# Adaptive-mix MoE feed-forward on one core: the shared branch's second layer in coarse and fine parts

## The chip, the cores and the metric

One core of a Trainium2 chip runs the whole program. The metric is device time in microseconds (us) of one execution. TensorE (PE) multiplies, VectorE (DVE), ScalarE (ACT) and GpSimd (POOL) do the elementwise work, SyncE (SP) issues most transfers. PEld is TensorE's weight load.

## The reference

There are 64 blocks of 32 rows by 512 features, so 2048 tokens. Each block's rows are first mixed by a small matrix that a conditioning network draws for it. The mixed rows xt then go through a mixture of experts with a shared branch:

```
logits = xt @ router_w + router_b            # 16 experts in 4 groups
gate   = top 2 experts per token, out of the best 2 groups
y      = sum over experts e of gate[:, e] * ((silu(xt @ w1[e] + b1[e]) * (xt @ w2[e] + b2[e])) @ w3[e] + b3[e])
z      = silu(xt @ sw1 + sb1) * (xt @ sw2 + sb2) @ sw3 + sb3      # the shared branch, 256 hidden
out    = x + y + z
```

All of it is float32. The change concerns the product with `sw3` alone, the shared branch's second layer: 2048 tokens x 256 hidden by 256 x 512.

## The kernel before, in words

Tokens are cut in 16 tiles of 128 and in 4 groups (g = 0 to 3) of 4 tiles. Each engine has one hand-written program, and semaphores join them; nothing is scheduled by a planner, so an engine's order is the order of the code.

1. *Mixing and routing (to about 58 us).* PE mixes and transposes the 16 tiles and forms the router's logits. For groups 0 and 1 and for the weights of the shared first layer, ACT copies each piece to a coarse part (type fp32r) and POOL subtracts that from the whole to get the fine part (line 454). These parts go into `x_split` and `w_split`.
2. *Shared first layer of groups 0 and 1 (58 to 80 us).* `shared_up(g, i)` on PE makes hidden block i (128 of the 256) of group g as three fp32r products for each pair of operands (coarse by coarse, coarse by fine, fine by coarse). ACT applies silu (`shared_silu`, line 808), DVE multiplies by the other half (`shared_hidden`, line 1014) and counts `up_ready` up. The result is `gs_of(g)`. Beside it DVE works out the gates and then each assignment's slot.
3. *Gates, shared second layer of the first tiles, dispatch (80 to 102 us).* PE transposes the gates, then `shared_down(0)` and tile 4 of `shared_down(1)`: for each tile two fp32 products of `gs_of(g)` with `sw3_sb` and one bf16 product with the bias rows. Then PE waits for DVE's and POOL's codes (lines 912 and 470) and makes the dispatch tables; then tiles 5 to 7, among the first transposes of gathered rows. DVE adds each finished tile (`shared_sum`, line 912), makes the tables of rows and the counts, and copies the first transposed rows (line 1129).
4. *Expert loop (102 to 209 us).* PE, DVE, ACT and POOL go through 34 tiles of assignments; POOL issues gathers (line 481) and scatters (line 487).
5. *End (209 to 257 us).* PE makes the shared first layer of groups 2 and 3 in plain fp32, then `shared_down(2)` and `shared_down(3)`. SP loads the experts' rows back. DVE's order is `shared_hidden(2)`, `add_rows(0)`, `add_rows(1)`, `shared_hidden(3)`, `add_rows(2)`, `shared_sum(2)`, `add_rows(3)`, `shared_sum(3)`. `add_rows` (line 1173) scales an expert's row by its gate and adds it: its two tensors both lie in SBUF. `shared_sum` has one tensor in SBUF and one in PSUM. For the last group ACT scales the second expert's rows (line 899) and POOL adds them (line 539).

## Time and profile before

| what | value |
|---|---|
| median of 3 runs | 260.02 us (259.42 to 263.33) |
| profiled execution | 259.11 us, span 257.2 us |
| PE busy | 241.2 us (94% of the span) |
| PE weight loads busy | 163.7 us (64%) |
| DVE busy | 148.5 us (58%) |
| POOL busy | 111.3 us (43%) |
| ACT busy | 78.7 us (31%) |

The span is the time between the first and the last event that the profiler shows; the execution's own time is 1.9 us longer. Busy shares are means over the stages above; the stages have different limits. A row of the timeline gives the start, the time to the end of the row, the engine, the line, what is written and read, and how many instructions the row holds; in square brackets stands how long the engine had been idle and what ended that.

### The profile page before, as it was taken

Reading aid. Unit: us, or ns where it says so; the run is one execution under the profiler, and the core shown is the slowest. Engines: PE = TensorE matmul, PEld = TensorE weight load, DVE = VectorE, ACT = ScalarE, POOL = GpSimd, SP = SyncE. Lnnn points to the kernel's source line nnn. Section 1 sums busy time; section 2 is a strip of 40 time slices with the busy share of each in tenths; the row PEclk is TensorE's granted clock in tenths of the full one; section 3 lists DMA queues with packets and bytes.
Section 4 is the critical chain, followed back from the end, with each engine's and each line's share of the span. In section 5 each row is a group of like instructions: output and inputs, shape, how many; then the busy total and the mean of one; then the engine's idle time right before and its main releaser. Section 6 shows DMA issues by size and latency. Waiting matters only on the chain.

```text
span 257.2 us, 3960 instructions
## 1 busy us (share of the span) xinstructions
PE 241.2 (94%) x1092; PEld 163.7 (64%) x1093; DVE 148.5 (58%) x314; ACT 78.7 (31%) x169; POOL 111.3 (43%) x135
## 2 busy tenths in 40 slices
PE   7947989899999988999999999999999999999994
PEld 6815767688877444667777777777777754444441
DVE  0599698838979979333333333334444420099895
ACT  2223345521317400233333333333333331100400
POOL 7782355421011056366666666666666331000170
PEclk9999799999999999999999999999999999999999
DMA  7998387689053946974445444455544222999965
GB/s 219 341 415 317 148 300 261 255 282 412 23 226 118 417 202 182 324 270 164 164 163 164 165 130 158 133 173 173 166 165 157 89 92 78 345 388 387 396 256 186
DMA packets 20698, 57.90 MB, mean 225 GB/s; under 512 B 2533, under 2 KB 2533, under 8 KB 20428
## 3 DMA queue, kind: packets, MB, share of 16 engines
q1 hardware_dynamic: 15084, 39.89, 42.2%
q0 software_dynamic: 5600, 17.83, 20.8%
q8 instruction: 7, 0.11, 0.2%
q14 instruction: 7, 0.06, 0.1%
HBM read 40.94 MB, written 17.30 MB: 226 GB/s over the span
## 4 chain that ended last, share of the span: by engine, by line
PE 78%; DVE 17%; issue 2%; DMA 1%; ACT 0%; DVEq 0%
PE psum L546 69%; PE psum L690 6%; DVE xT L1173 3%; DVE r L943 3%; DVE xT L912 2%; DVE xT L938 2%; PE psum L589 2%; DVE xT L953 2%; PE psum L703 2%; DMA xT<-cond_pack 1%; DVE x_early L912 1%; DVE mix_bias L940 1%; DVE xt_sb L1173 1%; DVE xt_sb L912 0%; DVE code_f L1107 0%
## 5 line engine op out<-in xcount | busy, mean ns | idle before, releaser
L546 PE MATMUL psum<-wexp,r 128*128 x272 | 68.4, 381 | 0.3 <-DVE r L1129 0.3
L546 PEld LDWEIGHTS psum<-wexp,r 128*128 128x128 f32 x272 | 48.5, 190 | 22.8 <-issue 16.8
L912 DVE TENSOR_TENSOR r<-psum,ebias 128x256 f32<-128x256 f32 x34 | 14.4, 425 | 65.0 <-PE psum L546 63.4
L487 POOL DMA_INDIRECT expert_rows<-late_region,to_row x33 | 33.4, 1011 | 33.6 <-ACT late_region L855 28.7
L481 POOL DMA_INDIRECT late_region<-xt_rows,from_row x36 | 35.3, 981 | 17.3 <-issue 10.8
L546 PE MATMUL psum<-wexp,xt_sb 128*128 x68 | 34.8, 594 | 0.0
L849 ACT ACTIVATE r<-r 128x128 f32<-128x128 f32 x34 | 10.5, 310 | 57.6 <-DVE r L912 47.6
L546 PE MATMUL psum<-xT,shared_sb 128*128 128x512 f32 x64 | 28.0, 593 | 0.0
L855 ACT ACTIVATE late_region<-psum 128x512 f32<-128x512 f32 x34 | 20.3, 598 | 13.9 <-issue 7.7
L1129 DVE COPY r<-psum 128x512 f32<-128x512 f32 x36 | 24.5, 680 | 0.0
L690 PE MATMUL psum<-ident,late_region 128*128 128x128 f32 x144 | 21.6, 273 | 1.0 <-DMA late_region<-xt_rows,from_row 1.0
L546 PE MATMUL psum<-x_split,w_split 128*128 128x512 f32 x96 | 22.3, 392 | 0.0
L546 PEld LDWEIGHTS psum<-xT,shared_sb 128*128 128x128 f32 x64 | 12.0, 190 | 15.5 <-issue 14.6
L690 PEld LDWEIGHTS psum<-ident,late_region 128*128 128x128 f32 x144 | 17.9, 141 | 5.5 <-issue 2.0
L546 PEld LDWEIGHTS psum<-x_split,w_split 128*128 128x128 f32 x96 | 17.9, 188 | 3.7
L791 ACT ACTIVATE xt_sb<-psum,mix_bias 128x512 f32<-128x512 f32 x16 | 11.0, 687 | 27.3 <-PE psum L546 14.2
L546 PE MATMUL psum<-router_sb,xT 128*128 128x16 f32 x128 | 16.2, 259 | 3.3 <-DVE xT L953 3.3
L546 PEld LDWEIGHTS psum<-router_sb,xT 128*128 128x128 f32 x128 | 16.0, 196 | 4.1 <-DVE xT L953 4.0
L454 POOL TENSOR_TENSOR x_split<-xT,x_split 128x512 fp32r<-128x512 f32 x8 | 10.2, 1279 | 14.3 <-ACT x_split L801 14.3
L953 DVE COPY xT<-psum 128x512 f32<-128x512 f32 x16 | 10.8, 690 | 7.5 <-PE psum L589 7.3
L539 POOL TENSOR_TENSOR xt_sb<-xt_sb,wexp 128x512 f32<-128x512 f32 x2 | 3.1, 1568 | 27.3 <-ACT wexp L899 27.3
L845 ACT ACTIVATE xt_sb<-psum 128x128 f32<-128x128 f32 x34 | 9.4, 278 | 15.1 <-PE psum L703 8.7
(175 smaller groups left out, 309.8 us busy)
## 6 DMA issues: line engine op xcount, KB each, us to landing
wexp<-expert_pack SPq DMA_DIRECT2D x16, 768.0 KB, 4.5
wexp<-expert_rows SPq DMA_DIRECT2D x8, 1024.0 KB, 13.1
xt_rows<-xt_sb SPq DMA_DIRECT2D x16, 256.0 KB, 2.2
x_early<-x SPq DMA_DIRECT2D x2, 1024.0 KB, 7.9
late_region<-x SPq DMA_DIRECT2D x2, 1024.0 KB, 12.5
ebias<-expert_bias SPq DMA_DIRECT2D x1, 2048.0 KB, 7.1
out_dram<-x_early SPq DMA_DIRECT2D x8, 256.0 KB, 9.3
shared_sb<-shared_pack SPq DMA_DIRECT2D x1, 1536.0 KB, 16.3
```

What stands on the lines that cost most here:

```text
L454: T.tensor_tensor(rest, whole, part, ALU.subtract).then_inc(split_ready, 1)
L481: nc.gpsimd.indirect_dma_start(out=xg[:, i % RING, :], out_offset=None, in_=xt_dram[:, :], in_offset=bass.IndirectOffsetOnAxis(ap=from_row ...
L487: nc.gpsimd.indirect_dma_start(out=y_dram[:, :], out_offset=bass.IndirectOffsetOnAxis(ap=rows_of.bitcast(U32), axis=0), in_=y_sb[:, slot, ...
L546: return nc.tensor.matmul(dst, lhsT, rhs, start=start, stop=stop)
L690: last = nc.tensor.transpose(psum[:, b, c * P:(c + 1) * P], xg[:, slot, c * P:(c + 1) * P], ident[:, :])
L791: nc.scalar.activation(xt_ring[:, t % RING, :], psum[:, t % 2, :], ACT.Identity, bias=mix_bias[:, t:t + 1]).then_inc(xt_ready, 1)
L849: nc.scalar.activation(s_sb[:, b, :], h_sb[:, b, 0, :], ACT.Silu).then_inc(s_ready, 1)
L855: nc.scalar.activation(y_sb[:, slot, :], psum[:, 6 + b, :], ACT.Copy).then_inc(y_ready, 1)
L912: return nc.vector.tensor_tensor(dst, a, b, op)
L953: V.tensor_copy(xT[:, t // GT, :, (t % GT) * P:(t % GT + 1) * P], psum[:, 2 + t % 2, :].rearrange("p (c n) -> p c n", c=C)).then_inc(xT_re ...
L1129: V.tensor_copy(xgT[:, b], psum[:, b, :].rearrange("p (c n) -> p c n", c=C)).then_inc(xgT_ready, 1)
L1173: ins = V.scalar_tensor_tensor(out=acc_tile(t), in0=rows_k[:, g, k, t % GT, :], scalar=tops[:, k, t:t + 1], in1=acc_tile(t), op0=ALU.mult, ...
```

## The change

The two fp32 products per tile of `shared_down` become six fp32r products. For each of the two hidden blocks: coarse hidden by coarse `sw3`, coarse hidden by fine `sw3`, fine hidden by coarse `sw3`. The bf16 bias product stays. The parts come from:

- `sw3_hi`: two ACT copies of 128x512, after ACT's exponential and ahead of its first silu; `sw3_lo`: two POOL subtractions, after the last of line 454.
- `gs_hi` of each group: two ACT copies of 128x512, after the gate parts (g = 0), after the last silu of group 1 (g = 1), after both silus of groups 2 and 3.
- `gs_lo` of each group: two POOL subtractions of 128x512; g = 0 and 1 ahead of POOL's share of the codes, g = 2 and 3 after its last scatter, ahead of its adds of line 539.

The parts are laid over regions that are free by then; `sw3_hi` is new memory, made free by a smaller scratch for POOL's transfers (8192 bytes of a partition in place of the default). `shared_down(g)` waits for its group's two fine blocks and for `sw3_lo`, where it had waited for `up_ready`.

```diff
--- before.py
+++ after.py
@@ -68,6 +68,20 @@
         with nc.sbuf_tensor("x_split", [P, EARLY, 2, C, GN], F32R) as x_split_sb, \
                 nc.sbuf_tensor("w_split", [P, 2, 2 * C * SHARED], F32R) as w_split_sb:
             x_split, w_split = x_split_sb[:, :, :, :, :], w_split_sb[:, :, :]
+        homes = {"wexp": 0, "ebias": 96, "shared_sb": 112, "x_early": 124, "late_region": 140, "xT": 156,
+                 "r1": 188, "xt_sb": 196}
+
+        def split_at(name, home, kb):
+
+            with nc.sbuf_tensor(f"ahead_of_{name}", [P, (homes[home] + kb) * 256], F32), \
+                    nc.sbuf_tensor(name, [P, IB, GN], F32R) as part:
+                return part[:, :, :]
+
+        gs_hi = (split_at("gs_hi0", "xT", 4), split_at("gs_hi1", "xT", 12), split_at("gs_hi2", "wexp", 68),
+                 split_at("gs_hi3", "late_region", 4))
+        gs_lo = (split_at("gs_lo0", "xt_sb", 0), split_at("gs_lo1", "xT", 8), split_at("gs_lo2", "wexp", 64),
+                 split_at("gs_lo3", "late_region", 0))
+        sw3_lo = split_at("sw3_lo", "shared_sb", 8)
         PRODUCTS = ((0, 0), (0, 1), (1, 0))
         w12_split = w_split.rearrange("p s (w c n) -> p s w c n", w=2, c=C)
         HALF = E // 2
@@ -161,6 +175,9 @@
                    + [spare[:, u * DIM:(u + 1) * DIM] for u in range(2)])
         gs_third = wexp_flat[:, NG * TOPK * GT * DIM:NG * TOPK * GT * DIM + IB * GN].rearrange(
             "p (i n) -> p i n", i=IB)
+
+
+        sw3_hi = sb("sw3_hi", [P, IB, DIM], F32R)
 
 
         ident = sb("ident", [P, P])
@@ -203,6 +220,10 @@
         half_loaded = [sem(f"half_loaded{h}") for h in range(2)]
         part_ready = sem("part_ready")
         split_ready = sem("split_ready")
+        down_part_ready = sem("down_part_ready")
+        down_split_ready = sem("down_split_ready")
+        gs_part_ready = sem("gs_part_ready")
+        gs_split_ready = [sem(f"gs_split_ready{g}") for g in range(NG)]
         b3_loaded = sem("b3_loaded")
         b3_ready = sem("b3_ready")
         consts_ready = sem("consts_ready")
@@ -452,6 +473,10 @@
                 pool.wait_ge(part_ready, u + 1)
                 whole, part, rest = split_of(u)
                 T.tensor_tensor(rest, whole, part, ALU.subtract).then_inc(split_ready, 1)
+            for i in range(IB):
+                pool.wait_ge(down_part_ready, i + 1)
+                T.tensor_tensor(sw3_lo[:, i, :], sw3_sb[:, i, :], sw3_hi[:, i, :], ALU.subtract
+                                ).then_inc(down_split_ready, 1)
             pool.wait_ge(xtT_done, NT)
             for r in range(RING):
                 pool.wait_ge(xt_stored[r], 16 * (NT // RING))
@@ -466,6 +491,13 @@
             pool.wait_ge(gate_rest_ready, 1)
             T.tensor_tensor(gate_rest, gate_rest, gate_parts[:, :, 1], ALU.subtract).then_inc(gate_rest_ready, 1)
 
+            def gs_rest(g):
+                for i in range(IB):
+                    pool.wait_ge(gs_part_ready, g * IB + i + 1)
+                    T.tensor_tensor(gs_lo[g][:, i, :], gs_of(g)[:, i, :], gs_hi[g][:, i, :], ALU.subtract).then_inc(gs_split_ready[g], 1)
+
+            gs_rest(0)
+            gs_rest(1)
             pool.wait_ge(code_base_ready, 1)
             T.tensor_tensor(tile_code[:, J_DVE:, 0, :], tile_code[:, J_DVE:, 0, :],
                             hi_code[:, J_DVE:].unsqueeze(2).to_broadcast([P, TOPK * NT - J_DVE, TW]), ALU.mult
@@ -532,6 +564,8 @@
             pool.wait_ge(to_copied, 1)
             scatter_rows(to_slot[:, 1:2], 1)
 
+            gs_rest(2)
+            gs_rest(3)
             pool.wait_ge(x_again_loaded, 16 * (NT - EARLY * GT))
             for u in range(GT):
                 t = LAST * GT + u
@@ -623,7 +657,8 @@
                             between[w, c]()
 
             def shared_down(g, tiles=range(GT)):
-                pe.wait_ge(up_ready, IB * (g + 1))
+                pe.wait_ge(down_split_ready, IB)
+                pe.wait_ge(gs_split_ready[g], IB)
                 for t in (g * GT + u for u in tiles):
                     if t == 0:
                         pe.wait_ge(gateT_ready, 1)
@@ -634,9 +669,12 @@
                     elif t in (6, 7):
                         pe.wait_ge(z_ready, t - 5)
                     bank = psum[:, DOWN_BANKS[t], :]
+                    cols = slice((t % GT) * P, (t % GT + 1) * P)
                     for i in range(IB):
-                        mm(bank, gs_of(g)[:, i, (t % GT) * P:(t % GT + 1) * P], sw3_sb[:, i, :],
-                           start=(i == 0), stop=False)
+                        whole, rest = gs_hi[g][:, i, cols], gs_lo[g][:, i, cols]
+                        mm(bank, whole, sw3_hi[:, i, :], start=(i == 0), stop=False)
+                        mm(bank, whole, sw3_lo[:, i, :], start=False, stop=False)
+                        mm(bank, rest, sw3_hi[:, i, :], start=False, stop=False)
 
                     if t == 0:
                         pe.wait_ge(b3_ready, 1)
@@ -812,6 +850,16 @@
             act.wait_ge(xtT_done, NT)
             for r in range(RING):
                 act.wait_ge(xt_stored[r], 16 * (NT // RING))
+            def gs_part(g):
+                for i in range(IB):
+                    act.wait_ge(up_ready, g * IB + i + 1)
+                    nc.scalar.activation(gs_hi[g][:, i, :], gs_of(g)[:, i, :], ACT.Copy
+                                         ).then_inc(gs_part_ready, 1)
+
+            act.wait_ge(shared_loaded, 16)
+            for i in range(IB):
+                nc.scalar.activation(sw3_hi[:, i, :], sw3_sb[:, i, :], ACT.Copy).then_inc(down_part_ready, 1)
+            act.wait_ge(split_ready, SPLITS)
             shared_silu(0)
             shared_silu(1, [0])
 
@@ -824,11 +872,13 @@
             nc.scalar.activation(gate_parts[:, :, 5], gate_parts[:, :, 0], ACT.Copy)
             act.wait_ge(gate_rest_ready, 2)
             nc.scalar.activation(gate_parts[:, :, 2], gate_rest, ACT.Copy).then_inc(gate_parts_ready, 1)
+            gs_part(0)
             for q in range(NG):
                 act.wait_ge(gateT_done, q + 1)
                 nc.scalar.activation(gateT[:, q * GN:(q + 1) * GN], psum[0:GROWS, GATE_BANKS[q], :], ACT.Copy
                                      ).then_inc(gateT_ready, 1)
             shared_silu(1, [1])
+            gs_part(1)
 
             act.wait_ge(pslot_ready, 1)
             act.wait_ge(gateT_done, NG)
@@ -890,7 +940,9 @@
             hidden_transposed(1, tiles)
             result(1, 1, tiles, count_of(act, N_SCATTERED + 2))
             shared_silu(2)
+            gs_part(2)
             shared_silu(3)
+            gs_part(3)
 
             act.wait_ge(rows_loaded[LAST], 16 * TOPK)
             for u in range(GT):
@@ -1193,7 +1245,7 @@
     import concourse.bacc as bacc
     from concourse.bass_utils import run_bass_kernel_spmd
 
-    nc = bacc.Bacc("TRN2", target_bir_lowering=False, num_devices=1)
+    nc = bacc.Bacc("TRN2", target_bir_lowering=False, num_devices=1, dynamic_dma_scratch_size=8192)
     a = {n.removeprefix("L0_").removeprefix("cond_"): np.asarray(v) for n, v in inputs.items()}
     cond, b2 = np.asarray(inputs["cond_128"]), a["b2"]
     _, out_c, in_c, _ = a["weight"].shape
```

POOL, from the last of `w_split` to the codes (before, then the change):

```order
L454 TENSOR_TENSOR w_split<-shared_sb,w_split 128x512 [waits part_ready] x4
L458 CAST xt_sb<-ebias 102x512 [waits xt_stored2,xt_stored1,xt_stored3,xt_stored0,xtT_done]
L459 CAST r<-ident 128x128
L460 IOTA xt_sb 128x128
L464 TENSOR_TENSOR late_region<-late_region 128x272 [waits gate_part_ready]
L467 TENSOR_TENSOR late_region<-late_region 128x272 [waits gate_rest_ready,gate_part_ready]
L470 TENSOR_TENSOR r<-r,hi_code 128x10x48 [waits code_base_ready]
```
```order
L475 TENSOR_TENSOR w_split<-shared_sb,w_split 128x512 [waits part_ready] x4
L478 TENSOR_TENSOR sw_lo<-shared_sb,sw_hi 128x512 [waits down_part_ready] x2
L483 CAST xt_sb<-ebias 102x512 [waits xt_stored2,xt_stored1,xt_stored3,xt_stored0,xtT_done]
L484 CAST r<-ident 128x128
L485 IOTA xt_sb 128x128
L489 TENSOR_TENSOR late_region<-late_region 128x272 [waits gate_part_ready]
L492 TENSOR_TENSOR late_region<-late_region 128x272 [waits gate_rest_ready,gate_part_ready]
L497 TENSOR_TENSOR gs_lo<-xt_sb,gs_hi 128x512 [waits gs_part_ready] x2
L497 TENSOR_TENSOR gs_lo<-xT,gs_hi 128x512 [waits gs_part_ready] x2
L502 TENSOR_TENSOR r<-r,hi_code 128x10x48 [waits code_base_ready]
```

Two subtractions for `sw3_lo` now stand ahead of the bias cast, and four for `gs_lo` ahead of the codes. The names of the tile read show the group: `xt_sb` holds group 0's hidden blocks, `xT` group 1's.

PE, from the gates' transposes into the second tile of `shared_down(0)` (before, then the change):

```order
L546 MATMUL psum<-r,late_region 102x128 [waits up_ready,ranks_read,ident_bf_ready,gate_parts_ready]
L546 MATMUL psum<-r,late_region 102x128 x15
L546 MATMUL psum<-shared_sb,xt_sb 128x512 [waits gateT_ready,up_ready]
L546 MATMUL psum<-shared_sb,xt_sb 128x512
L546 MATMUL psum<-xt_sb,xT 128x512 [waits b3_ready]
L546 MATMUL psum<-shared_sb,xt_sb 128x512 [waits gateT_ready]
L546 MATMUL psum<-shared_sb,xt_sb 128x512
```
```order
L580 MATMUL psum<-r,late_region 102x128 [waits up_ready,ranks_read,ident_bf_ready,gate_parts_ready]
L580 MATMUL psum<-r,late_region 102x128 x15
L580 MATMUL psum<-sw_hi,gs_hi 128x512 [waits gateT_ready,gs_split_ready0,down_split_ready]
L580 MATMUL psum<-sw_lo,gs_hi 128x512
L580 MATMUL psum<-sw_hi,gs_lo 128x512
L580 MATMUL psum<-sw_hi,gs_hi 128x512
L580 MATMUL psum<-sw_lo,gs_hi 128x512
L580 MATMUL psum<-sw_hi,gs_lo 128x512
L580 MATMUL psum<-xt_sb,xT 128x512 [waits b3_ready]
L580 MATMUL psum<-sw_hi,gs_hi 128x512 [waits gateT_ready]
```

Where the first tile began with `up_ready`, it now waits for the fine parts of the hidden blocks and of `sw3`, and has six products ahead of its bias product.

POOL, from its last scatter to the end (before, then the change):

```order
L531 ISA [waits y_ready]
L531 COPY to_slot<-to_row 128x1
L487 DMA expert_rows<-late_region,to_slot 4096x512 [waits to_copied]
L539 TENSOR_TENSOR xt_sb<-xt_sb,wexp 128x512 [waits last_scaled,x_again_loaded]
L539 TENSOR_TENSOR xt_sb<-xt_sb,wexp 128x512 [waits last_scaled]
L539 TENSOR_TENSOR xT<-xT,wexp 128x512 [waits last_scaled] x2
```
```order
L563 ISA [waits y_ready]
L563 COPY to_slot<-to_row 128x1
L519 DMA expert_rows<-late_region,to_slot 4096x512 [waits to_copied]
L497 TENSOR_TENSOR gs_lo<-wexp,gs_hi 128x512 [waits gs_part_ready] x2
L497 TENSOR_TENSOR gs_lo<-late_region,gs_hi 128x512 [waits gs_part_ready] x2
L573 TENSOR_TENSOR xt_sb<-xt_sb,wexp 128x512 [waits last_scaled,x_again_loaded]
L573 TENSOR_TENSOR xt_sb<-xt_sb,wexp 128x512 [waits last_scaled]
L573 TENSOR_TENSOR xT<-xT,wexp 128x512 [waits last_scaled] x2
```

The four subtractions of groups 2 and 3 come ahead of the four adds.

## Rows read from the trace of the kernel before

**Rows 1.** The page: the chain that ended last, share of the span by engine.
```profile
PE 78%; DVE 17%; issue 2%; DMA 1%; ACT 0%; DVEq 0%
```

**Rows 2.** Chain of waits from 56 to 103 us: start, us, what.
```profile
81.44 9.92 PE psum L546 x25
...
92.10 1.53 PE psum L546 x32
...
101.82 1.34 PE psum L546 x5
```

**Rows 3.** Timeline of TensorE: fp32r products, then fp32 products (two records each).
```profile
74.71 5.73 PE L546 MATMUL psum<-x_split,w_split 128*128 128x512 f32 x24
...
212.80 25.05 PE L546 MATMUL psum<-xT,shared_sb 128*128 128x512 f32 x58
```

**Rows 4.** Timeline from 57 to 92 us: VectorE, GpSimd and ScalarE on slots and codes.
```profile
57.80 0.61 POOL L458 CAST xt_sb<-ebias 102x512 bf16<-102x512 f32 x1 [4.85 <-DMA xt_rows<-xt_sb]
...
60.87 0.42 DVE L912 TENSOR_TENSOR late_region<-late_region,r 128x256 f32<-128x256 f32 x1
...
74.99 0.42 DVE L1045 COPY late_region<-psum 128x256 f32<-128x256 f32 x1 [1.41 <-PE psum L546]
...
78.39 0.46 ACT L826 ACTIVATE late_region<-late_region 128x272 bf16<-128x272 f32 x1
...
79.07 0.59 DVE L912 TENSOR_TENSOR late_region<-psum,late_region 128x256 f32<-128x256 f32 x1
...
84.19 3.35 DVE L912 TENSOR_TENSOR late_region<-xt_sb,pslot 128x3072 bf16<-128x3072 bf16 x1
...
87.45 1.75 DVE L912 TENSOR_TENSOR r<-tile_iota,late_region 128x1536 bf16<-128x1536 f32 x1
...
89.94 2.06 POOL L470 TENSOR_TENSOR r<-r,hi_code 128x480 bf16<-128x480 bf16 x1 [11.59 <-DVE r L1082]
```

**Rows 5.** Timeline near 20 us: a subtraction on GpSimd, four copies on VectorE.
```profile
18.50 0.78 DVE L943 COPY r<-xT 32x64 f32<-32x64 f32 x4
...
21.91 1.29 POOL L454 TENSOR_TENSOR x_split<-xT,x_split 128x512 fp32r<-128x512 f32 x1 [3.35 <-ACT x_split L801]
...
21.98 1.87 DVE L943 COPY r<-xT 32x64 f32<-32x64 f32 x4
```

**Rows 6.** Instructions of lines 801 and 1173: ns min/median/max, first and last start.
```profile
L801 ACT ACTIVATE x_split<-xT x8: 619/620/631, 21.1 to 41.1; 128x512 fp32r<-128x512 f32 x8
...
L1173 DVE SCALAR_TENSOR_TENSOR x_early<-wexp,tops,x_early x16: 746/747/752, 226.1 to 236.3; 128x512 f32<-128x512 f32 x16
L1173 DVE SCALAR_TENSOR_TENSOR xT<-wexp,tops,xT x10: 743/747/1762, 239.3 to 251.2; 128x512 f32<-128x512 f32 x10
```

**Rows 7.** Timeline of the end, 224 to 254 us.
```profile
224.88 0.75 DVE L1014 SCALAR_TENSOR_TENSOR wexp<-psum,router_sb,wexp 128x512 f32<-128x512 f32 x1 [6.12 <-ACT wexp L808]
...
238.61 0.75 DVE L1014 SCALAR_TENSOR_TENSOR late_region<-psum,router_sb,late_region 128x512 f32<-128x512 f32 x1 [0.87 <-ACT late_region L808]
...
243.17 3.10 POOL L539 TENSOR_TENSOR xt_sb<-xt_sb,wexp 128x512 f32<-128x512 f32 x2 [27.35 <-ACT wexp L899]
...
245.06 1.75 DVE L1173 SCALAR_TENSOR_TENSOR xT<-wexp,tops,xT 128x512 f32<-128x512 f32 x1
...
246.23 2.95 POOL L539 TENSOR_TENSOR xT<-xT,wexp 128x512 f32<-128x512 f32 x2
...
246.85 2.48 DVE L912 TENSOR_TENSOR xT<-xT,psum 128x512 f32<-128x512 f32 x4
...
252.96 0.38 PE L546 MATMUL psum<-xt_sb,xT 102*128 102x512 bf16 x1
253.22 1.28 DVE L912 TENSOR_TENSOR xT<-xT,psum 128x512 f32<-128x512 f32 x2
```

**Rows 8.** Stretches of mixing: length, busy us (PE, PEld, DVE, ACT, POOL), PEclk, DMA share, GB/s.
```profile
22.00:25.20 3.20, 1.66 (x11) 1.08 (x10) 3.10 (x8) 1.29 (x2) 1.20 (x1) 1.00 0.89 284
25.20:28.60 3.40, 3.40 (x13) 2.26 (x12) 2.61 (x7) 0.67 (x3) 1.27 (x1) 0.50 0.52 208
```

## The prediction

> **What bounds the kernel now.** The page's chain of what ended last gives TensorE 78% and VectorE 17% [rows 1], so a cheaper product looks like pure gain. I then read the chain in order of time, where the change is. TensorE works without a gap from 81.44 to 91.36 us, but the dispatch starts at 92.10 [rows 2]. It does not wait for TensorE's products: GpSimd's part of the codes runs from 89.94 to 92.00, and was released by VectorE [rows 4]. VectorE itself was last kept waiting by TensorE at 74.99 (1.41 us idle before it), and works almost without a gap from there through the slots' 3.35 us, the codes' 1.75 us and on [rows 4]. So from 75 to 92 us **VectorE sets the pace**. After the dispatch the same holds: TensorE enters the expert loop at 101.82, when VectorE's copy has come [rows 2]. The timeline of the end shows it a second time. TensorE releases ScalarE, and that VectorE, for the last hidden block at 238.61. From there VectorE does eight scaled adds, four sums, four scaled adds and four sums on end. TensorE's last product ends at 253.34, just as VectorE is busy with the last but one sum (its last two run from 253.22 to 254.50) [rows 7]. A faster second layer is not what VectorE waits for there either.
>
> **TensorE's part.** An fp32r record of 128x512 costs 5.73 / 24 = 0.24 us, an fp32 one 25.05 / 58 = 0.43, and an fp32 product has two of these [rows 3]. For each tile, four records of 0.43 (1.73) become six of 0.24 (1.43): 0.3 us less, with nearly the same number of weight loads beside them. Over 16 tiles that is 4.8 us of TensorE's time. I count none of it. Tiles 0 to 4 end 1.5 us sooner in front of the codes, which come at 92.0 whatever TensorE does; tiles 5 to 7 lie beside VectorE's tables; tiles 8 to 15 lie beside VectorE's adds [rows 2, 4, 7].
>
> **What the parts cost.** ScalarE makes ten copies of 128x512 at 0.62 us [rows 6] and GpSimd ten subtractions at 1.29 us [rows 5]. ScalarE's are hidden: the two of `sw3` fall after its exponential, where it waits for the first hidden block; the others come when it would be idle. Its one-hots stand behind group 1's copies and so come later by A and B below and two copies, 3.3 us, the dispatch that needs them by 4.2. The bias cast, and the transfer of the experts' biases behind it in SyncE's queue, come some 5 us later than 57.80 [rows 4], and are first needed in the loop at 101.82 [rows 2].
>
> GpSimd's subtractions are not hidden from VectorE. At 21.91 GpSimd subtracts; the four copies that VectorE begins at 21.98 take 1.87 us in place of 0.78 [rows 5], 1.09 more. At the end an add of line 1173, both tensors in SBUF, takes 1.75 and 1.76 us beside GpSimd's adds where it takes 0.75 alone [rows 6, 7], 1.01 more. The four sums that read PSUM, beside GpSimd's third and fourth add, take 2.48 together, 0.62 each: nothing more [rows 7]. So **an operation of VectorE with both tensors in SBUF, and one of GpSimd, take turns**, and each turn of GpSimd costs VectorE about 1.05 us. They alternate: two adds of GpSimd held up two adds of VectorE. I now place all ten subtractions.
>
> - A, `sw3` (2). ScalarE's exponential is done before VectorE's row at 60.87 uses it, so with a copy behind it they run from about 60.8, in the gate chain, whose operations of 0.42 us mostly have both inputs in SBUF [rows 4]. 2 x 1.05 = 2.1, less the 1.41 us for which VectorE idles before 74.99: **0.7**. Bounds: 0, if they fall between those operations; 1.6, if the casts that now follow them (0.61 and 0.30) block too.
> - B, group 0 (2). ScalarE's gate parts end at 78.85, a copy later GpSimd starts, 79.5. VectorE is then in an operation from PSUM (79.07 to 79.66 before, now moved by A to 80.4), so the first costs 0.35, the second 1.05: **1.4**. Bounds 0.4 and 2.1.
> - C, group 1 (2). They start when VectorE has made group 1's hidden blocks, that is, together with its slots of 3.35 us and then its codes of 1.75 us, all from SBUF [rows 4]. Whoever is first, two turns are taken before GpSimd can do its codes: **2.1**. Bounds 1.0 and 2.2.
> - D, group 2 (2). The hidden block is done at 225.63 [rows 7]; GpSimd runs from 225.5 into the 16 adds that begin at 226.1 [rows 6]: 0.5 + 1.05, less the 0.87 us idle before 238.61 [rows 7]: **0.7**. Bounds 0 and 1.2.
> - E, group 3 (2). They fall in the eight adds after 239.3: **2.1**. Bounds 1.0 and 2.2.
> - F, GpSimd's old adds (4). Two of them met adds of VectorE, two met sums from PSUM and were free [rows 7]. Those eight adds now begin 0.7 later and give two turns to E, so they are still running until about 251 and meet all four: **2.1** more. Bounds 0 and 2.2.
>
> Also moved: TensorE starts `shared_down(0)` at about 82.3 in place of 81.44, since it waits for group 0's second subtraction; tiles 0 to 3 are done long before the codes, and no one waits for them. Tile 4 waits for group 1's second subtraction, at 92 to 94 us, and ends before the codes, which now come at 96.2 (92.0 + A + B + C). At the end group 3's subtractions are done by 243.5, before TensorE reaches tile 12.
>
> Sum: 0.7 + 1.4 + 2.1 = 4.2 before the loop, 0.7 + 2.1 + 2.1 = 4.9 behind it, 9.1 in all. Against the profiled execution's 259.1 that gives 268.2; the median of the runs shown, 260.0, lies 0.9 above that execution. I take the middle, **268.7 us**. The bounds of the terms together give 2.4 to 11.5: 261.5 to 271.5.
>
> The Trainium skill ("SBUF — State Buffer", section "SBUF: two separate sides") says that the pair of ports that VectorE and GpSimd share is locked for a whole instruction and that the loser blocks fully. By the Trainium skill a turn would be the subtraction's whole 1.29 us; with the ten full turns of A to F that makes 2.4 us more, 271.1, the upper edge of the forecast's case. The rows show 1.01 and 1.09 at the places where a turn was taken [rows 5, 6], so the trace agrees that the loser waits, and not on how long; my sum goes by the rows.
>
> **Rivals.** (1) *Turns are taken, but in fewer places*: long operations of VectorE keep GpSimd out until a free place comes, or only one of the two stages is hit. For it: the sums from PSUM are such places. Against: an add behind an add was held up each time. About half the sum: 262 to 265. (2) *No turn costs anything*, the subtractions fall into VectorE's gaps or its idle 1.41 and 0.87 us. Then nothing on the path has changed: 259 to 260. Against it stand rows 5 to 7. (3) *TensorE is the bound, as the page's chain has it*, and its 4.8 us come off: 260.0 - 4.8 = 255, and with the shorter record, without the tail of the last, up to 1 us less, 254. It decides if VectorE keeps up behind TensorE's last products, which 253.34 beside 253.22 seems to allow [rows 7]; but VectorE's sums there are the end of a queue of its own and not released one by one. (4) *TensorE's clock*. In 22.00 to 25.20 TensorE was busy for 1.66 of 3.20 us, and the next 3.40 us ran at half the clock, 1.2 GHz [rows 8]. Between tile 3 (at 89) and tile 4 (at up to 94) TensorE now idles as long. If its clock falls, 3.4 us of its work take 6.8; it has some 2 us of room until the gathered rows come, so up to 1.5 us more: 270 to 272. (5) *The smaller scratch* holds up GpSimd's gathers or scatters in the loop. No row before shows such a hold. From below it costs nothing; upward it is open, since a hold of only 0.1 us on each of the 34 tiles, if nothing covered it, would be 3.4. I take nothing, since each tile's transfers have a whole turn of the loop, (209 - 102) / 34 = 3.1 us, and keep a small chance for more than 271.
>
> **Chances.** The forecast's sum (265.2 to 271) 0.67; rival 1, 0.13; rival 2, 0.12; rival 3, 0.03; rivals 4 and 5 together 0.05. A measurement of this kernel can tell about 2%, that is 254.8 to 265.2. Faster than that: 0.03, rival 3. Within: rivals 1 and 2, 0.25. Slower: 0.72. The range leaves out rivals 2 and 3 and most of 4 and 5: 262 to 271.
>
> **What would show it.** After: fp32r records of the second layer at 0.24 us or below; two of VectorE's gate operations near 61 to 64 us and two in the slots or codes lengthened by 1.0 each; the dispatch at 96 us, the loop's first product at 106; five or six adds of line 1173's counterpart in `add_rows(2)` at 1.7 us in place of two; TensorE idle before the dispatch and done 3 us or more before VectorE's last sum. I am wrong if the dispatch starts before 94 us, or if VectorE's adds at the end keep their 0.75 beside GpSimd's subtractions.

## The result and the profile after

The changed kernel took **274.09 us** (median of 4, 272.26 to 278.88), the kernel before beside it 259.72 (4 runs): 1.0559 times as long, 95% interval 1.0452 to 1.0666. The forecast was 268.7 with a range to 271. The profiled execution took 273.99 us with a span of 271.6, 14.9 and 14.4 more than before. (A few medians below include runs in which the whole core ran slower for no reason of the kernel's; ratios and intervals leave those out.)

The page's chain, by engine, beside [rows 1]:

```profile
PE 51%; DVE 33%; DMA 5%; issue 5%; POOL 3%; another core or an unknown queue 1%; DVEq 1%; ACT 1%; SPq 0%; POOLq 0%
```

VectorE has twice its former share, GpSimd appears, and "issue", time in which an engine waits for nothing that the profile shows, went from 2% to 5%. The first two fit the forecast, the last was not in it.

**Ahead of the loop.** The timeline of the changed kernel at `sw3` (A), at group 0 (B) and at group 1 (C):

```profile
59.74 2.72 POOL L478 TENSOR_TENSOR sw_lo<-shared_sb,sw_hi 128x512 fp32r<-128x512 f32 x2 [8.89 <-ACT sw_hi L861]
59.91 1.40 DVE L964 TENSOR_TENSOR late_region<-late_region,r 128x256 f32<-128x256 f32 x1
61.34 1.40 DVE L964 TENSOR_TENSOR late_region<-late_region,router_sb 128x256 f32<-128x256 f32 x1
...
78.02 2.51 POOL L497 TENSOR_TENSOR gs_lo<-xt_sb,gs_hi 128x512 fp32r<-128x512 f32 x2 [1.07 <-ACT gs_hi L856]
78.31 0.07 DVE L1105 MEMSET r<- 128x16 f32 x1
78.41 0.95 DVE L1106 TENSOR_TENSOR_SCAN count<-r,count 128x16 f32<-128x16 f32 x1
79.39 1.17 DVE L964 TENSOR_TENSOR count<-count 128x16 f32<-128x16 f32 x1
...
85.91 3.35 DVE L964 TENSOR_TENSOR late_region<-xt_sb,pslot 128x3072 bf16<-128x3072 bf16 x1
86.08 7.04 POOL L497 TENSOR_TENSOR gs_lo<-xT,gs_hi 128x512 fp32r<-128x512 f32 x2 [5.54 <-ACT gs_hi L856]
89.17 2.82 DVE L964 TENSOR_TENSOR r<-tile_iota,late_region 128x1536 bf16<-128x1536 f32 x1
92.03 1.50 DVE L1134 TENSOR_SCALAR r<-r,part_iota 128x1536 bf16<-128x1536 bf16 x1
93.26 0.47 PE L580 MATMUL psum<-sw_hi,gs_hi 128*128 128x512 f32 x1 [3.87 <-POOL gs_lo L497]
...
95.78 2.35 PE L580 MATMUL psum<-r,late_region 128*128 128x96 bf16 x32
```

Each pair of subtractions lengthens exactly two operations of VectorE. The gate operations take 1.40 us in place of 0.42 [rows 4]. The scan and the difference behind it have only 16 elements for each partition, and take 0.95 and 1.17. The code table takes 2.82 in place of 1.75 [rows 4], and the operation behind it 1.50. Before, these three small ones took 0.19, 0.18 and 0.62, the last in this row:

```profile
89.24 0.62 DVE L1082 TENSOR_SCALAR r<-r,part_iota 128x1536 bf16<-128x1536 bf16 x1
```

This last one reads a single large tensor, with one number for each partition beside it, and is held up all the same. So is a copy with one input, 0.73 us in place of 0.29, that now runs beside a GpSimd operation of the gates (75.01 us). GpSimd's two subtractions of group 1 need 7.04 us, since the first waits behind the slots' 3.35. Tile 4 starts at 93.26, and the 3.87 us that TensorE idles before it are what rival 4 feared: the dispatch's 32 products take 2.35 us for 1.53 [rows 2]. The windows view (columns as in [rows 8]) has the clock:

```profile
88.00:93.20 5.20, 1.39 (x7) 0.70 (x5) 5.17 (x3) 2.05 (x5) 5.11 (x2) 1.00 0.80 334
94.10:97.60 3.50, 3.50 (x29) 2.46 (x28) 1.92 (x3) 0.00 (x0) 1.57 (x1) 0.51 0.02 5
```

TensorE was busy for 1.39 of 5.20 us at the full 2.4 GHz, and then worked at 1.2.

**The loop and its exit.** VectorE's rows at the 28th tile of the loop, and TensorE's at the last tile and behind it (the timeline):

```profile
193.59 0.42 DVE L964 TENSOR_TENSOR r<-psum,ebias 128x256 f32<-128x256 f32 x1 [1.80 <-PE psum L580]
...
198.61 0.42 DVE L964 TENSOR_TENSOR r<-psum,ebias 128x256 f32<-128x256 f32 x1 [3.81 <-remote]
```

```profile
213.93 1.02 PE L580 MATMUL psum<-wexp,xt_sb 128*128 x2
...
217.66 3.34 PE L580 MATMUL psum<-xT,shared_sb 128*128 128x512 f32 x4 [2.70 <-issue]
```

Before, `shared_up(2)` begins as soon as the last tile's down product is through, and its first four records take 1.96:

```profile
208.12 1.02 PE L546 MATMUL psum<-wexp,xt_sb 128*128 x2
209.18 1.96 PE L546 MATMUL psum<-xT,shared_sb 128*128 128x512 f32 x4
```

So one tile took 5.02 us, where the same one took 3.25 before. At the exit TensorE stood for 2.70 us and waited for nothing that the profile shows ("issue"). Its clock fell meanwhile:

```profile
215.00:217.60 2.60, 0.00 (x0) 0.00 (x0) 0.03 (x1) 0.59 (x1) 0.98 (x1) 0.89 0.21 76
217.60:220.50 2.90, 2.84 (x4) 1.32 (x5) 0.00 (x0) 0.00 (x0) 0.00 (x0) 0.51 0.24 90
```

**The end**, beside [rows 7]:

```profile
235.31 2.94 POOL L497 TENSOR_TENSOR gs_lo<-wexp,gs_hi 128x512 fp32r<-128x512 f32 x2 [9.62 <-ACT gs_hi L856]
235.51 12.83 DVE L1225 SCALAR_TENSOR_TENSOR x_early<-wexp,tops,x_early 128x512 f32<-128x512 f32 x16
...
249.57 11.60 DVE L1225 SCALAR_TENSOR_TENSOR xT<-wexp,tops,xT 128x512 f32<-128x512 f32 x8
249.74 3.43 POOL L497 TENSOR_TENSOR gs_lo<-late_region,gs_hi 128x512 fp32r<-128x512 f32 x2 [11.48 <-ACT gs_hi L856]
...
253.12 3.44 POOL L573 TENSOR_TENSOR xt_sb<-xt_sb,wexp 128x512 f32<-128x512 f32 x2
...
256.52 3.43 POOL L573 TENSOR_TENSOR xT<-xT,wexp 128x512 f32<-128x512 f32 x2
...
260.24 0.39 PE L580 MATMUL psum<-xt_sb,xT 102*128 102x512 bf16 x1
261.20 2.48 DVE L964 TENSOR_TENSOR xT<-xT,psum 128x512 f32<-128x512 f32 x4
```

Six operations of GpSimd now meet `add_rows(2)`, whose eight adds take 11.60 us. TensorE is done at 260.63, before VectorE begins its last twelve operations. The row of that line beside [rows 6] (ns min/median/max):

```profile
L1225 DVE SCALAR_TENSOR_TENSOR xT<-wexp,tops,xT x10: 739/1717/1784, 249.6 to 265.6; 128x512 f32<-128x512 f32 x10
```

**Where the 14.4 us went**, from the starts of the same work in the two traces: the mixing stage gave 0.95 back; A cost 0.5; B and C 3.7 and the small pieces, mostly the copy named above, 0.4 up to the dispatch; the clock there 0.7; the tile at 193.6 us 1.4 (the next step gave part back); the exit's wait 2.7; the clock behind it 1.4; D 0.45; E and F 4.1. (The sum is 14.4 with rounding.) The turns, the small pieces with them, are 9.1 us, against 9.1 forecast. The miss is the other part, and most of it is at the exit.

### The profile page after: what moved, and what is told of

Read it like the earlier page. It is cut to its first block, busy times and chain, and to the rows that moved or that the text cites. A ratio compares the mean times of both kernels' runs of the same rounds, so it can differ in the third digit from the quotient of the medians.

```text
span 271.6 us, 4048 instructions
## 1 busy us (share of the span) xinstructions
PE 238.4 (88%) x1124; PEld 168.9 (62%) x1125; DVE 161.2 (59%) x314; ACT 84.3 (31%) x179; POOL 130.3 (48%) x145
## 4 chain that ended last, share of the span: by engine, by line
PE 51%; DVE 33%; DMA 5%; issue 5%; POOL 3%; another core or an unknown queue 1%; DVEq 1%; ACT 1%; SPq 0%; POOLq 0%
PE psum L580 43%; DVE late_region L964 5%; PE psum L728 5%; DVE x_early L1225 4%; DVE xT L1225 4%; DVE r L995 3%; DMA wexp<-expert_rows 3%; POOL gs_lo L497 3%; DVE xT L964 3%; DVE xT L990 2%; PE psum L623 2%; DVE xT L1005 2%; PE psum L741 1%; DMA xT<-cond_pack 1%
## 5 line engine op out<-in xcount | busy, mean ns | idle before, releaser
L964 DVE TENSOR_TENSOR r<-psum,ebias 128x256 f32<-128x256 f32 x34 | 14.4, 425 | 66.3 <-PE psum L580 62.5
L580 PE MATMUL psum<-xT,shared_sb 128*128 128x512 f32 x64 | 29.4, 617 | 2.7 <-issue 2.7
L580 PE MATMUL psum<-sw_hi,gs_hi 128*128 128x512 f32 x32 | 15.5, 484 | 4.0 <-POOL gs_lo L497 3.9
```

The lines of the kernel that those rows point to most:

```text
L580: return nc.tensor.matmul(dst, lhsT, rhs, start=start, stop=stop)
L964: return nc.vector.tensor_tensor(dst, a, b, op)
```

## The experiments

The theory for the miss: TensorE's program is longer. A product in fp32 is four instructions (two loads and two products, as it has two records of each). One in fp32r or bf16 is two, and so is a transposition, which has one record of each. So 48 for 16 in front of the loop are 32 instructions more, and two waits come to them. At the exit TensorE jumps over the pairs of tiles that this routing lacks, and the place behind them has to be in a block of the program that was fetched. The page's row of the queue that carries these blocks gives their size, 0.13 MB / 8 = 16 KB:

```profile
q8 instruction: 8, 0.13, 0.2%
```

By the Trainium skill ("Runtime: NRT & Kernel Launch", section "Instruction fetch mechanics") a block of 16 KiB holds 256 instructions, two are held, and a taken branch to a place outside them forces a fetch that execution waits for. (The same section also gives TensorE room for 2048 instructions.) Counted in the compiled program, the place behind the loop is instruction 1767 before and 1801 after the change, on either side of 1792 = 7 x 256. No trace shows these numbers. What the traces show is the queue. Before, a packet of q8 starts 0.4 us after the last down product does, and the next one 4.75 us later, when TensorE is long back at work. In the change the two start at 214.27 and 217.36, and TensorE's first product at 217.66: the idle time lies between two blocks. It is the same in the five runs below that have an idle time there of 2.78 us or more (experiments 1, 3, 5, 10 and 11): the second packet comes 3.1 to 3.4 us after the first, the product 0.3 to 0.4 behind it.

**1. No subtractions.** GpSimd's ten subtractions go, the products stay. The kernel leaves out the fine parts, and TensorE waits for the coarse ones instead.

```diff
-            gs_rest(0)
-            gs_rest(1)
...
-                        whole, rest = gs_hi[g][:, i, cols], gs_lo[g][:, i, cols]
+                        whole, rest = gs_hi[g][:, i, cols], gs_hi[g][:, i, cols]
-                        mm(bank, whole, sw3_lo[:, i, :], start=False, stop=False)
+                        mm(bank, whole, sw3_hi[:, i, :], start=False, stop=False)
```

> The change without GpSimd's ten subtractions: the products read the coarse parts three times, so the number of TensorE's products, ScalarE's ten copies and the program's length stay. It leaves out the fine parts. Theory (turn-taking costs 9.3 us, the rest of the loss is a wait of TensorE for its program at the end of the expert loop and the half clock behind it): about 265 us; the idle time of TensorE before the first product of shared_up(2) stays at 2.7 us. Rival (everything comes from the turn-taking, the stall too, since it shifts the phase): about 260 us or under, with an idle time of 0.8 us there.

Measured: 265.04 us (263.82 to 266.8), 1.0261 times before [1.0159, 1.0362]; 9.05 us below the change by the medians, 8.9 by the spans. The exit's idle time is still there (2.8 us), so is the long tile (4.9). The 16 and the eight adds of rows take what they took before:

```profile
231.12 10.94 DVE L1217 SCALAR_TENSOR_TENSOR x_early<-wexp,tops,x_early 128x512 f32<-128x512 f32 x16
...
244.75 7.58 DVE L1217 SCALAR_TENSOR_TENSOR xT<-wexp,tops,xT 128x512 f32<-128x512 f32 x8
```

What follows: the turns are worth 9 us in this kernel, and the stall is not theirs. (Two smaller differences nearly cancel: the dispatch's half clock, 0.7, goes with the subtractions, and of the 0.95 that the change gained in the mixing stage this kernel has 0.25.)

**2. The parts unused.** Copies and subtractions as in the change, products in fp32 as before.

```diff
-                        mm(bank, whole, sw3_hi[:, i, :], start=(i == 0), stop=False)
-                        mm(bank, whole, sw3_lo[:, i, :], start=False, stop=False)
-                        mm(bank, rest, sw3_hi[:, i, :], start=False, stop=False)
+                        mm(bank, gs_of(g)[:, i, cols], sw3_sb[:, i, :],
+                           start=(i == 0), stop=False)
```

> The other half: ScalarE's ten copies and GpSimd's ten subtractions as in the change (the difference is written over the coarse part, which no product reads), and TensorE's fp32 products as before. Theory: 269 us (9.3 us of turns) and an idle time of 0.8 us at the exit of the expert loop, since TensorE's program is as long as before. Rival (the stall comes with GpSimd's or ScalarE's part): 273 to 274 us with the idle time of 2.7 us.

Measured: 269.42 us (268.24 to 270.99), 1.0402 [1.0308, 1.0497], and no idle time at the exit (TensorE's timeline):

```profile
215.65 1.02 PE L580 MATMUL psum<-wexp,xt_sb 128*128 x2
216.71 1.95 PE L580 MATMUL psum<-xT,shared_sb 128*128 128x512 f32 x4
```

So the change's losses split by engine: the turns come with GpSimd's part, the exit with TensorE's products. Here tile 4, in fp32, holds the dispatch up too: the dispatch starts at 97.91, GpSimd's codes end at 97.17.

**3. The kernel before, 32 instructions longer.**

```diff
             keep_warm(8)
+            for _ in range(8):
+                mm(psum[:, 7, 0:1], ident[:, :], ident[:, 0:1])
 
 
             for s in range(NT + 2):
```

> The kernel before with eight products of one column more ahead of the mixing stage, 32 instructions of TensorE (as many as the change adds ahead of the loop). Theory (the place of the loop's exit in the instruction blocks decides): idle time at the exit 2.7 us for 0.8 us and the half clock behind it, 263 to 264 us. Rival (the stall has nothing to do with the program's length): 259.7 to 260.5 us, idle time 0.8 us.

Measured: 264.7 us (263.57 to 265.52), 1.0231 [1.0137, 1.0325]. Eight products of one column cost 5.8 us, 200 us after they ran. TensorE's rows at the exit, and the windows behind it:

```profile
207.75 1.02 PE L546 MATMUL psum<-wexp,xt_sb 128*128 x2
211.84 3.75 PE L546 MATMUL psum<-xT,shared_sb 128*128 128x512 f32 x4 [3.06 <-issue]
```

```profile
212.00:215.00 3.00, 3.00 (x4) 1.21 (x5) 0.00 (x0) 0.00 (x0) 0.00 (x0) 0.50 0.14 52
215.00:218.00 3.00, 3.00 (x6) 1.26 (x5) 0.00 (x0) 0.28 (x1) 0.00 (x0) 0.54 0.00 0
```

**4. The change, 32 instructions shorter**, with the same columns in its warming products.

```diff
-            keep_warm(8)
+            keep_warm_wide(2, 4)
             pe.wait_ge(masks_ready, 1)
...
+            def keep_warm_wide(products, times):
+                for _ in range(products):
+                    mm(psum[:, 7, 0:times * P].rearrange("p (u n) -> p u n", u=times), ident[:, :],
+                       ident[:, :].unsqueeze(1).to_broadcast([P, times, P]))
```

(Four of the first products became two of twice the width in the same way.)

> The change with twelve of TensorE's 128-column warming products made as four wide ones, 32 instructions fewer for the same number of columns; the loop's exit then stands in the instruction blocks where it stood before the change. Theory: idle time at the exit 0.8 us, full clock behind it, 270 us. Rival: 274 us and 2.7 us as in the change.

Measured: 272.59 us (269.18 to 275.41), 1.0445 [1.0322, 1.0568]. By the ratios that is some 3 us below the change, but the intervals overlap, so the time shows little and the trace has to. The exit is as clear as in 2: the last down product starts at 219.94, `shared_up(2)` at 221.00, four records in 1.96 us. Experiments 3 and 4 add and take away the stall with TensorE's warming products alone.

**5. Instructions that never run.** The eight products of 3 now stand in the branch that this routing never takes.

```diff
             with pe.If(pairs > SURE + 2):
+                keep_warm(8)
                 with pe.Fori(1, (PAIRS - SURE) // 2) as j:
```

> The kernel before with eight products more inside the last branch of the expert loop, which this routing never takes: TensorE executes not one instruction more, but the place behind the loop moves 32 instructions on, from 32 ahead of a 256-instruction boundary (counted from the program's start) onto it. Theory (the exit's jump lands in a block that has not been fetched): TensorE idle 2.7 to 3.1 us at the exit, half clock behind it, 263.5 to 265 us. Rival (the eight executed products of the padded kernel did it, by clock or phase): 259 us and no idle time.

Measured: 261.24 us (10 runs, 259.97 to 267.77), 1.0077 [1.0034, 1.0120]. The wait is there as expected:

```profile
207.81 1.02 PE L546 MATMUL psum<-wexp,xt_sb 128*128 x2
211.88 1.95 PE L546 MATMUL psum<-xT,shared_sb 128*128 128x512 f32 x4 [3.05 <-issue]
```

But the clock behind it stayed up (four records in 1.95 us where 3 has 3.75), and so the loss is 2.0 to 2.5 us and not five. The idle times are the same to a hundredth, 3.05 and 3.06. Of the 3.5 us between the medians of 3 and 5 the clock makes 2.9: TensorE comes back at 211.84 and 211.88, and begins its next long stretch, `shared_up` in 58 records, at 218.39 and 215.50. The idle time alone doesn't decide that the clock falls. What does is open.

**6. Half the pad**, four products, 16 instructions: the place behind the loop is 1783, still in the block ahead of 1792.

```diff
+            for _ in range(4):
+                mm(psum[:, 7, 0:1], ident[:, :], ident[:, 0:1])
```

> The kernel before with four executed products of one column more, 16 instructions: the place behind the loop stays in the block that has been fetched, 16 instructions ahead of its end. Theory: no idle time at the exit, at most half a microsecond where TensorE runs into the next block, 258.5 to 259.5 us. Rival (any pad costs, or a pad costs in proportion): 261 to 262 us.

Measured: 260.3 us (10 runs, 258.86 to 265.2), 1.0084 [1.0034, 1.0134]. The theory said no idle time, and there is 1.82:

```profile
206.14 1.02 PE L546 MATMUL psum<-wexp,xt_sb 128*128 x2
208.98 1.45 PE L546 MATMUL psum<-xT,shared_sb 128*128 128x512 f32 x3 [1.82 <-issue]
```

So "is the target in a fetched block" is not the whole rule. The exit is two jumps: over the 18th pair, which is absent, and over the branch with the rest. My refined theory: in 6 the first jump enters a new block, before it doesn't; and whatever jump comes while a block is on its way waits, 1.8 us if its target is at hand, 2.7 to 3.1 us if it isn't. The record doesn't bear out its first half. By the count above the first jump goes from 1485 to 1571 before and from 1501 to 1587 in 6, both across 1536. And the queue is the same in both: a packet of q8 starts 0.35 us after the last down product does, at 208.47 for 208.12 before and at 206.49 for 206.14 in 6. What 6 waits for stays open.

**7. A pad six times as long**: 48 products of one column, 192 instructions, in the mixing stage.

```diff
                     mm(psum[:, s % 2, :], mixT[:, s, :], x_tile(s)).then_inc(xt_done, 1)
+                    for _ in range(3):
+                        mm(psum[:, 7, 0:1], ident[:, :], ident[:, 0:1])
```

> The kernel before with three products of one column behind each of the sixteen mixing products, 192 instructions, six times what cost 5.5 us. Theory as the last runs left it (a jump waits where a block of instructions is still on its way; with 16 instructions more the first jump at the exit enters a new block and the second waits 1.8 us, with 32 the second also leaves it and waits 3.1): with 192, TensorE enters that block some 78 instructions ahead of the first jump, 4 to 5 us, so it has landed and no jump waits: no idle time at the exit, full clock behind it. The products themselves lengthen the mixing stage by 0 to 5 us, which is read there. Rival (the longer the code the longer the wait): 3 us or more idle at the exit.

Measured at the exit: no idle time.

```profile
252.70 1.02 PE L546 MATMUL psum<-wexp,xt_sb 128*128 x2
253.67 1.97 PE L546 MATMUL psum<-xT,shared_sb 128*128 128x512 f32 x4
```

"Longer is worse" falls. But that the refined theory forecast it is luck: it had TensorE enter a block 4 to 5 us ahead of the first jump, and q8 has no packet between 168.40 and 253.36 us. By the count, the first jump now stays in its block, and the second goes from 1764 to 1959, into the block that was asked for when the loop first ran past 1536, at 168.4. A simpler rule is enough for all runs but 6: entering a block asks for the next, and a jump into a block asked for just before (the change, 3 and 5) waits for it. No run tests this rule.

As a whole the kernel is no measurement: one execution took 262.88 us, three 301.65 to 304.75. The page of one of those three has TensorE's granted clock, in 40 slices:

```profile
PEclk9985555555555599999999999999999999999999
```

From the mixing stage until past the dispatch it is 1.2 GHz, with TensorE busy most of that time. (The mean clock of the other two, 0.85 and 0.86, is that of this one.) That was not expected, and no run here explains it.

**8. The smaller scratch alone.**

```diff
-    nc = bacc.Bacc("TRN2", target_bir_lowering=False, num_devices=1)
+    nc = bacc.Bacc("TRN2", target_bir_lowering=False, num_devices=1, dynamic_dma_scratch_size=8192)
```

> The kernel before with the scratch of the dynamic DMAs at 8192 for its default, and nothing else. In the four kernels with that scratch the tile step at 28 took 4.9 to 5.0 us for 3.1 to 3.3. Theory (the scratch does it): one step of 4.9 us here too, no idle time at the exit, 260.5 to 261 us. Rival (the step comes from ScalarE's or GpSimd's new instructions or the buffers' places): no step above 3.6 us, the time within 0.7 us of before.

Measured: 259.65 us (258.26 to 264.82), 1.0050 [0.9993, 1.0107]. The long tile is there, at the same tile as in the change:

```profile
193.43 0.42 DVE L912 TENSOR_TENSOR r<-psum,ebias 128x256 f32<-128x256 f32 x1 [1.80 <-PE psum L546]
...
198.50 0.42 DVE L912 TENSOR_TENSOR r<-psum,ebias 128x256 f32<-128x256 f32 x1 [3.85 <-remote]
```

**9. A scratch of 4096.**

> The kernel before with a quarter of the default scratch of the dynamic DMAs. Theory (with 8192 the scratch is used up once, at tile 28, and GpSimd or a queue waits until it is free; with 4096 that comes earlier and again): two to three tile steps of about 5 us, near tiles 12 to 14 and 28, 261 to 263 us. Rival (the long step at tile 28 has another cause): at most the one at tile 28, 259 to 260.5 us.

Measured: 260.03 us (10 runs), 1.0042 [0.9994, 1.0090]. One long tile, the 14th in place of the 28th, 4.46 us, and none later:

```profile
144.51 0.42 DVE L912 TENSOR_TENSOR r<-psum,ebias 128x256 f32<-128x256 f32 x1 [1.80 <-PE psum L546]
...
148.96 0.42 DVE L912 TENSOR_TENSOR r<-psum,ebias 128x256 f32<-128x256 f32 x1 [3.23 <-PE psum L546]
```

Of the eight kernels with 8192 seven had the long tile at the 28th, in one (11) the longest step, the 29th, took 3.67 us. Half the scratch, half the tiles until the hold: the scratch sets its place. That it comes back was wrong. What it costs is too little for these runs to tell from nothing; with the step behind it, which is shorter than before, the traces show 1.4 us at 8192 and 1.1 at 4096.

**10. Copies for subtractions**: GpSimd with one input in place of two.

```diff
-                    T.tensor_tensor(gs_lo[g][:, i, :], gs_of(g)[:, i, :], gs_hi[g][:, i, :], ALU.subtract).then_inc(gs_split_ready[g], 1)
+                    T.tensor_copy(gs_lo[g][:, i, :], gs_hi[g][:, i, :]).then_inc(gs_split_ready[g], 1)
```

> The change with GpSimd's ten subtractions made as ten copies of the coarse part, one input for two (the fine parts are left out). Theory (a VectorE operation with two SBUF tensors takes turns with any GpSimd operation, however many inputs that has): the gate operations and the adds of rows under them are still lengthened, each by about the copy's length, and if a copy is as long as a subtraction, 273 to 274 us. Rival (GpSimd too must read two tensors): 265 us as without them, VectorE's operations at 0.42 and 0.71 us under the copies.

Measured: 268.29 us (266.55 to 269.62), 1.0399 [1.0342, 1.0456], between the two: 3.3 us above no subtractions, 5.8 below the change. The timeline at `sw3`:

```profile
59.64 1.37 POOL L478 CAST sw_lo<-sw_hi 128x512 fp32r<-128x512 f32 x2 [8.87 <-ACT sw_hi L861]
59.83 0.70 DVE L964 TENSOR_TENSOR late_region<-late_region,r 128x256 f32<-128x256 f32 x1
60.57 0.72 DVE L964 TENSOR_TENSOR late_region<-late_region,router_sb 128x256 f32<-128x256 f32 x1
```

The two gate operations are still held up, by 0.3 us each and not by 1.0, and group 1's two copies still wait behind the slots (5.75 us together). So GpSimd takes a turn with one input too, and of two lengths tried, a turn's price follows the length of GpSimd's operation: 0.3 us for a copy of 0.69, 1.0 for a subtraction of 1.3. Both theories were wrong here, each by half.

**11. VectorE subtracts** itself.

```diff
+            def gs_rest(g):
+                for i in range(IB):
+                    dve.wait_ge(gs_part_ready, g * IB + i + 1)
+                    tt(gs_lo[g][:, i, :], gs_of(g)[:, i, :], gs_hi[g][:, i, :], ALU.subtract).then_inc(gs_split_ready[g], 1)
...
             add_rows(2)
+            gs_rest(3)
```

> The change with the ten subtractions on VectorE itself, at places where ScalarE has made the coarse part. Theory: each costs VectorE its own length, 0.7 us, for the 1.05 us of a turn: seven us for 9.3, and GpSimd's four adds meet six or seven sums as before; the loop's exit and tile 28 stay as in the change: 271 to 272 us. Rival (the turns in the change cost less than it looks, since VectorE then waits less for others): 274 us or more.

Measured: 273.33 us (269.92 to 274.79), 1.0514 [1.0441, 1.0586], against 1.0559 for the change: no difference that can be told. A pair takes 1.29 us on VectorE where two turns cost 2.1, but the last pair met GpSimd's adds and took 3.30, and the last two sums waited 0.23 and 0.93 us for TensorE. Handing the subtractions to an "idle" GpSimd relieved VectorE of nothing.

**12. Groups 2 and 3 alone.** The early groups keep fp32, `sw3` is split behind the loop.

```diff
                     for i in range(IB):
+                        if g < 2:
+                            mm(bank, gs_of(g)[:, i, cols], sw3_sb[:, i, :],
+                               start=(i == 0), stop=False)
+                            continue
```

> The change for groups 2 and 3 alone; groups 0 and 1 keep the fp32 products, and the second weights are split behind the expert loop, since the fine part is written over them. Theory: E and F as in the change (4.1 us), D about 0.5, the two subtractions of the weights now meet the adds of the result, 2.1, and 1.4 at tile 28 if the scratch gives it: 267 to 268 us. TensorE's program ahead of the loop is that of before, so no idle time of 2.7 us at the loop's exit. Rival (the stall comes from the code behind the loop or from other engines): 271 us and the idle time there.

Measured: 264.96 us (264.84 to 265.11), 1.0274 [1.0244, 1.0305]. TensorE's program is as long as the change's behind the loop and as before ahead of it, and there is no idle time at the exit: what counts is how much stands ahead of the exit, not the length of the whole. The two subtractions of `sw3` ran at 217.17 in 2.51 us while VectorE was idle, so they were free, where 2.1 had been expected. The rest (12.49 us for the 16 adds, 11.58 for the eight, the long tile) is that of the change.

## Why the prediction was wrong, and where it was right

- **What bounds the kernel**: right. TensorE is done 8.2 us ahead of the end of VectorE's last sum, and its cheaper products bought nothing: a tile takes 1.61 us for 1.94. Ahead of the dispatch it was closer than the prediction had it. TensorE waited 3.87 us for tile 4's fine part, and this tile, most of it at half clock, ended at 95.84, about when GpSimd's codes did (95.67); there was no room left.
- **The ten turns**: right, in mechanism, place and nearly in size. 4.6 ahead of the loop for 4.2 forecast (A 0.5 for 0.7; B and C 3.7 for 3.5; small pieces 0.4), 4.5 behind it for 4.9 (D 0.45 for 0.7; E and F together 4.1 for 4.2, six of eight adds lengthened, the median of that line's adds 1.72 us for 0.75). Experiment 1 gives 9 us for all. The rule of the Trainium skill ("SBUF — State Buffer", section "SBUF: two separate sides") would have made it 11.5, an estimate; the traces show 0.8 to 1.1 us for a turn. What I had taken for a constant follows the length of GpSimd's operation (experiment 10). And "with both tensors in SBUF" was read too narrowly for inputs: the copies of [rows 5] that gave the price have one input, and two operations with one input were held up again.
- **The dispatch** came at 95.78 for 96, the loop's first product at 106.23 for 106.
- **What failed: TensorE's part, where the change's extra instructions had no term.** The step reads "nearly the same number of weight loads beside them ... I count none of it", and that the products are hidden is true. But 32 instructions more ahead of the loop moved the place behind its exit: 2.7 us of waiting and 1.4 of half clock (experiments 1 to 5 and 12). That the place costs the time is shown, by 5 above all; that it does so by a block that has to be fetched is argued, from the count and from the packets of q8. With `shared_up(2)` at the exit all that VectorE does at the end starts later; no cover stands there. This is 4.1 of the 5.4 us by which the forecast missed; the rest is the two rivals below, 0.7 and 1.4, less the 0.95 that the mixing stage gave back.
- **Rival 4, the clock**: I priced it at up to 1.5 us and gave it and rival 5 together 0.05. It came at its place with 0.7, and a second time at the exit.
- **Rival 5, the scratch**: I took nothing. A hold came, but at one tile and not at each, 1.4 us in the traces (experiments 8 and 9); its share in the time is not settled by the runs.
- **The bounds** were too narrow for a sum to which three things can be added that don't depend on the turns. With each of 1 to 4 us, the upper end belonged at 276.

No version here is faster than the kernel before. The best of the change's parts (12) costs 2.7%, and shortening the program (4) only gives back what the length took.

## What to carry to other kernels

Before work is moved to GpSimd, look at which operations of VectorE run beside it: each one with two inputs in SBUF waited for one operation of GpSimd, however small it was itself, and so did some with one (0.62 us became 1.50, 0.29 became 0.73); those that read PSUM didn't. In a program with a loop of variable length or skipped branches, an edit that adds instructions anywhere ahead can cost 1.6 to 6 us at the exit (experiments 3, 5, 6); if the profile shows "issue" in front of the first instruction behind a loop, shift the code by some products and look again, before the edit itself is judged. And when TensorE's products get cheaper off the path, ask what they leave idle: the clock may fall there.

## What was not expected of the hardware

- The two jumps at the loop's exit cost nothing, 1.82 us of idle time or 2.7 to 3.1, by where the place behind the loop stands: nothing as before and with 192 instructions more ahead of it, 1.82 with 16, 3.1 with 32 (experiments 3 and 5 to 7).
- Eight products, 32 instructions, that never run cost 2.0 us of 259, 0.77% [0.34, 1.20].
- After the same idle time (3.05 and 3.06 us) TensorE's granted clock stayed at 1.00 in one kernel and fell to 0.50 for some 6 us in another. The medians of the two kernels are 3.5 us apart.
- With 48 products of one column more in the mixing stage, three executions of four took over 301 us and one 262.88. In the profiled one of the three the clock was at 1.2 GHz for more than 70 us; why is open.
- VectorE's 16-element operations, 0.19 and 0.18 us long before, were held to 0.95 and 1.17 by GpSimd's subtraction as the large ones were.
